# Expert stage of layer 0: an expert's 640 rows as units of 384 and 256 rows in place of twice 320

## What is computed

```python
capacity = max(1, int(T * CAPACITY_FACTOR / E))      # 2048 * 1.25 / 8 = 320
probs_full = jax.nn.softmax(xt @ Wr, axis=-1)
topv, topi = jax.lax.top_k(probs_full, TOPK)         # TOPK = 2
topv = topv / jnp.sum(topv, axis=-1, keepdims=True)
onehot = jax.nn.one_hot(topi, E, dtype=x.dtype)
rank = jnp.cumsum(onehot, axis=0)                    # per choice and expert
keep = (rank <= capacity).astype(x.dtype) * onehot
w = jnp.einsum('tk,tke->te', topv, keep)
h = jax.nn.gelu(jnp.einsum('td,edf->etf', xt, W1) + b1[:, None, :], approximate=False)
y = jnp.einsum('etf,efd->etd', h, W2) + b2[:, None, :]
out = jnp.einsum('te,etd->td', w, y)
```

## Time and profile before

| | us |
|---|---|
| median of three runs | 2173.74 |
| the three runs | 2163.47, 2173.74, 2173.80 |
| profiled execution, its own time | 2166.46 |
| its span, first to last instruction | 2164.7 |
| stage of the change, from the first `up` matmul to the first gather | 576.6 to 669.7 |

### The profile page before, as it was taken

The page is one execution under the profiler, slowest core; times in us unless marked ns, Lnnn a source line. Parts: engine busy times, 40 slices in busy tenths (PEclk is TensorE's granted clock), DMA queues, the critical chain, the costliest instruction groups (busy, mean ns, idle before and its releaser), DMA issues.

```text
span 2164.7 us, 31890 instructions
## 1 busy us (share of the span) xinstructions
PE 1946.3 (90%) x9894; PEld 1233.9 (57%) x9894; DVE 1432.5 (66%) x3907; ACT 966.6 (45%) x2009; POOL 1236.1 (57%) x1608
## 2 busy tenths in 40 slices
PE   5999999999794799999999988989699999898975
PEld 3655555555593465655655556777455555554554
DVE  6698688887243766666666544445578888876733
ACT  1445445444443435544544533545234445444443
POOL 1569977777453346766767700011256676798743
PEclk8899999999897889999999989999799999999987
DMA  5245132221423324434434220000312223222233
GB/s 138 65 108 146 46 81 50 59 58 41 136 74 82 73 59 103 98 75 98 98 79 93 65 81 20 1 12 1 80 43 70 53 52 84 61 66 71 54 102 97
DMA packets 126354, 155.59 MB, mean 72 GB/s; under 512 B 22136, under 2 KB 66456, under 8 KB 125928
## 3 DMA queue, kind: packets, MB, share of 16 engines
q1 hardware_dynamic: 121832, 145.43, 27.0%
q0 software_dynamic: 4352, 8.12, 1.2%
HBM read 47.84 MB, written 17.40 MB: 30 GB/s over the span
## 4 chain that ended last, share of the span: by engine, by line
PE 61%; DVE 12%; POOL 11%; issue 9%; ACT 4%; DMA 1%; SPq 0%; POOLq 0%; DVEq 0%; ACTq 0%
PE P L796 60%; POOL acc L1534 4%; POOL yd L1551 3%; DVE P L1924 2%; POOL xg L1542 1%; POOL acc L1531 1%; DVE mx L1913 1%; POOL pr L1512 1%; ACT pr L1302 1%; DMA xg<-xs,sidx 1%; DVE qB L1889 1%; DVE bst L1828 1%; PE P L823 0%; DVE mx L1924 0%; DVE mx L1934 0%
## 5 line engine op out<-in xcount | busy, mean ns | idle before, releaser
L1534 POOL TENSOR_TENSOR acc<-acc,pr 128x512 f32<-128x512 f32 (+3 forms) x768 | 676.5, 904 | 94.4 <-ACT pr L1302 70.1
L1302 ACT ACTIVATE pr<-P 128x512 f32<-128x512 f32 (+1 forms) x768 | 396.5, 567 | 398.3 <-PE P L796 388.7
L796 PE MATMUL P<-pr,vt 128*64 128x512 f32 (+3 forms) x2304 | 445.0, 507 | 5.1 <-POOL pr L1512 5.0
L796 PE MATMUL P<-qA,kA 128*128 128x512 f32 (+2 forms) x1024 | 413.1, 406 | 31.4 <-ACT pr L1302 31.0
L796 PE MATMUL P<-qB,kB 128*128 128x512 f32 (+2 forms) x1024 | 370.7, 367 | 0.0
L1512 POOL TENSOR_SCALAR_AFFINE_SELECT pr<-pr 128x256 f32<-128x256 f32 x384 | 156.7, 408 | 342.1 <-ACT pr L1302 305.1
L796 PEld LDWEIGHTS P<-qA,kA 128*128 128x128 f32 x1024 | 195.0, 190 | 160.6 <-issue 73.3
L796 PEld LDWEIGHTS P<-pr,vt 128*64 128x64 f32 x2304 | 146.8, 139 | 233.8 <-issue 195.5
L1913 DVE TENSOR_REDUCE mx<-P 128x1 f32<-128x512 f32 x384 | 243.8, 683 | 44.4 <-PE P L796 43.0
L1531 POOL TENSOR_TENSOR acc<-pr,pr 128x384 f32<-128x384 f32 x192 | 217.6, 1144 | 87.4 <-ACT pr L1302 87.2
L1924 DVE CUSTOM_DVE_ANT_0 P<-P,maskQ,mx 128x512 f32<-128x512 f32 (+3 forms) x384 | 190.0, 554 | 45.4 <-PE P L796 44.4
(11 more groups left out here) (331 smaller groups left out, 3196.4 us busy)
## 6 DMA issues: line engine op xcount, KB each, us to landing
qA<-hq SPq DMA_DIRECT2D x384, 128.0 KB
kA<-stage SPq DMA_DIRECT2D x168, 128.0 KB
qB<-qB SPq DMA_DIRECT2D x96, 128.0 KB
kB<-stage SPq DMA_DIRECT2D x84, 128.0 KB
nr<-null_share SPq DMA_DIRECT2D x64, 128.0 KB, 2.9
yd<-in_c_zero SPq DMA_DIRECT2D x32, 128.0 KB, 2.7
w<-in_L_W SPq DMA_DIRECT2D x16, 256.0 KB, 5.8
xg<-xg SPq DMA_DIRECT2D x24, 129.0 KB
```

Of the source, the lines that this page charges most:

```text
L796: return P.matmul(out, lhs, rhs, start=start, stop=stop)
L1302: S.activation(a.pr[slot][:, r, 512 - wide:512], m.bank[b][:, 512 - wide:512], AF.Exp, scale=0.125).then_inc(s.free[b], 1)
L1534: G.tensor_tensor(acc[:, sl], acc[:, sl], pt[:, sl], ALU.add).then_inc(s.acc, 1)
```

## The change

An expert's 640 rows stay where they are, with the same weights. Unit 2e now takes the first 384 of them, unit 2e+1 the last 256. The row tiles of a unit are then 128, 128, 128 or 128, 128. The third transpose, the third group of four `down` matmuls, the third part of the index and bias operations, the third scatter and the second row load exist for even units only. `up`, its Gelu and the `xt` copies have 384 or 256 columns. The `xt` and `h` buffers grow from 320 to 384 columns. The tables of the destinations, `c_base0` and `c_place0`, are made as before (with 320 rows for each unit), and so are all sizes of layer 3, whose counts of semaphores are only written in another form.

```diff
--- before.py
+++ after.py
@@ -15,7 +15,8 @@
...
 ROWS = {0: 16 * L0_CAP, 3: 8 * L3_CAP}
-CAP = {0: L0_CAP, 3: L3_CAP}
+SHARES = {0: (384, 256), 3: (L3_CAP,)}
 UNITS = {0: 16, 3: 8}
@@ -27,6 +28,19 @@
...
           3: (("Wq", 0, 512, "wq"), ("Wq", 512, 512, "wq"), ("Wk", 0, 64, "wk"))}
+
+def share(L, u):
+    return SHARES[L][u % len(SHARES[L])]
+
+def first_row(L, u):
+    return u // len(SHARES[L]) * sum(SHARES[L]) + sum(SHARES[L][:u % len(SHARES[L])])
+
+def row_tiles(L, u):
+    return [(o, min(128, share(L, u) - o)) for o in range(0, share(L, u), 128)]
 
@@ -579,7 +593,7 @@
...
     def experts(stack, L):
-        e, W, per = Box(), CAP[L], UNITS[L] // 8
+        e, W, per = Box(), max(SHARES[L]), UNITS[L] // 8
         e.raw = [sb(stack, f"w1raw{i}", [128, 512]) for i in range(3)]
@@ -1001,32 +1015,31 @@
...
                 L, u = k
-                W = CAP[L]
                 w.wait_ge(s.x_rows[u % 5], rows_count(L, u))
...
                 xg = m.E[L].xg[u % 5]
-                for t, (o, wd) in enumerate(((0, 128), (128, 128), (256, W - 256))):
+                for t, (o, wd) in enumerate(row_tiles(L, u)):
                     last = P.transpose(ps[:, o:o + wd], xg[0:wd, t, 0:D], m.ident[0:wd, 0:wd])
...
                 L, u, mt = k
-                e, W = m.E[L], CAP[L]
+                e, W = m.E[L], share(L, u)
                 ex = u // (UNITS[L] // 8)
...
                 ms = slice(mt * 128, mt * 128 + 128)
-                mm3(ps[:, 0:W], e.w1[ex % 4][0][:, ms], e.w1[ex % 4][1][:, ms], e.xt[u % 3][0][:], e.xt[u % 3][1][:],
+                mm3(ps[:, 0:W], e.w1[ex % 4][0][:, ms], e.w1[ex % 4][1][:, ms], e.xt[u % 3][0][:, 0:W], e.xt[u % 3][1][:, 0:W],
                     True, True).then_inc(s.full[b], 1)
...
                 L, u = k
-                e, W = m.E[L], CAP[L]
+                e = m.E[L]
                 ex = u // (UNITS[L] // 8)
...
                 w.wait_ge(s.free[b], uses)
-                for t, (o, wd) in enumerate(((0, 128), (128, 128), (256, W - 256))):
+                for t, (o, wd) in enumerate(row_tiles(L, u)):
                     for kk in range(4):
@@ -1165,7 +1178,8 @@
...
 
-    return 32 * (u // 5 + 1 + (0 if L == 0 else len([v for v in range(16) if v % 5 == u % 5])))
+    units = [(l, v) for l in (0, 3) for v in range(UNITS[l]) if v % 5 == u % 5 and (l, v) <= (L, u)]
+    return sum(32 if share(*unit) > 256 else 16 for unit in units)
 
@@ -1361,7 +1375,7 @@
...
                     w.wait_ge(*pl.filled("up", L, u - 3, 3))
-                S.copy(m.E[L].xt[u % 3][0][:].bitcast(FR), ps[:, 0:CAP[L]]).then_inc(s.e_x, 1)
+                S.copy(m.E[L].xt[u % 3][0][:, 0:share(L, u)].bitcast(FR), ps[:, 0:share(L, u)]).then_inc(s.e_x, 1)
             elif kind == "up":
@@ -1369,7 +1383,7 @@
...
                     w.wait_ge(*pl.filled("down", L, u - 3))
-                S.activation(e.h[u % 3][:, mt, :], ps[:, 0:CAP[L]], AF.Silu if L else AF.Gelu,
+                S.activation(e.h[u % 3][:, mt, 0:share(L, u)], ps[:, 0:share(L, u)], AF.Silu if L else AF.Gelu,
                              bias=e.b1[:, ex * 4 + mt:ex * 4 + mt + 1]).then_inc(s.free[b], 1)
@@ -1547,7 +1561,7 @@
...
                 w.wait_ge(s.e_to, od.nth("cols", L, u))
-                for t, wide in enumerate((128, 128, CAP[L] - 256)):
+                for t, (_, wide) in enumerate(row_tiles(L, u)):
                     G.indirect_dma_start(yd[L], bass.IndirectOffsetOnAxis(ap=e.ni[u % 4][0:wide, t:t + 1], axis=0),
@@ -1572,7 +1586,8 @@
...
 
-    return 48 * (u // 4 + 1 + (0 if L == 0 else 4))
+    units = [(l, v) for l in (0, 3) for v in range(UNITS[l]) if v % 4 == u % 4 and (l, v) <= (L, u)]
+    return sum(16 * len(row_tiles(*unit)) for unit in units)
 
@@ -1582,9 +1597,10 @@
...
     def rows_in(xg, L, u, sem):
-        W = CAP[L]
-        Y.dma_start(xg[:, 0:2, :], xgd[L][u * W:u * W + 256, :].rearrange("(t p) d -> p t d", p=128)).then_inc(sem, 16)
-        Y.dma_start(xg[0:W - 256, 2, :], xgd[L][u * W + 256:u * W + W, :]).then_inc(sem, 16)
+        o, W = first_row(L, u), share(L, u)
+        Y.dma_start(xg[:, 0:2, :], xgd[L][o:o + 256, :].rearrange("(t p) d -> p t d", p=128)).then_inc(sem, 16)
+        if W > 256:
+            Y.dma_start(xg[0:W - 256, 2, :], xgd[L][o + 256:o + W, :]).then_inc(sem, 16)
 
@@ -2159,14 +2175,14 @@
...
                 L, u = k
-                e, W = m.E[L], CAP[L]
+                e, W = m.E[L], share(L, u)
                 xg = e.xg[u % 5]
...
                     w.wait_ge(s.y_out[u % 4], y_count(L, u - 4))
-                parts = ((128, slice(0, 2)), (W - 256, slice(2, 3)))
+                parts = ((128, slice(0, 2)), (W - 256, slice(2, 3)))[:1 + (W > 256)]
                 for wd, c in parts:
@@ -2179,17 +2195,19 @@
...
                 w.wait_ge(s.e_x, od.nth(*item))
-                V.tensor_tensor(e.xt[u % 3][1][:].bitcast(FR), ps[:, 0:W], e.xt[u % 3][0][:], ALU.subtract).then_inc(s.free[b], 1)
+                V.tensor_tensor(e.xt[u % 3][1][:, 0:W].bitcast(FR), ps[:, 0:W], e.xt[u % 3][0][:, 0:W], ALU.subtract).then_inc(s.free[b], 1)
             elif kind == "down":
                 L, u = k
-                e, W = m.E[L], CAP[L]
+                e, W = m.E[L], share(L, u)
                 ex, y = u // (UNITS[L] // 8), e.y[u % 4]
...
                     w.wait_ge(s.y_out[u % 4], y_count(L, u - 4))
-                V.tensor_tensor(y[:, 0:2, :], ps[:, 0:256].rearrange("p (i n) -> p i n", i=2),
-                                e.b2[:, ex:ex + 1, :].broadcast_to([128, 2, 128]), ALU.add)
-                V.tensor_tensor(y[0:W - 256, 2, :], ps[0:W - 256, 256:384], e.b2[0:W - 256, ex, :], ALU.add).then_inc(s.free[b], 1)
+                last = V.tensor_tensor(y[:, 0:2, :], ps[:, 0:256].rearrange("p (i n) -> p i n", i=2),
+                                       e.b2[:, ex:ex + 1, :].broadcast_to([128, 2, 128]), ALU.add)
+                if W > 256:
+                    last = V.tensor_tensor(y[0:W - 256, 2, :], ps[0:W - 256, 256:384], e.b2[0:W - 256, ex, :], ALU.add)
+                last.then_inc(s.free[b], 1)
             elif kind == "comb":
```

## The result

The changed kernel takes 2156.52 us (median of 16 runs), beside 2166.53 us for the kernel before (16 runs on the same chip): a ratio of 0.9951, interval 0.9937 to 0.9965, so 10 us or 0.5% less. The forecast of 2157.7 is 1.2 us off, and that is luck: I took 16 us off the median of three runs, 2173.7, the median of sixteen lies 7 us lower, and the gain came out 6 us smaller. The two misses cancel.

The account below looks back on a forecast made before the run. PE was taken to bound the stage from the first `up` to the last `down`; 9.5 + 4.1 + 1.4 - 0.35 - 0.1 + 1.3 = 15.85, say 16 us, off 2173.74 gave 2157.7 us, range 2145 to 2168.

Parts of the forecast that it names:

- `down`, 9.5 us: `down` matmuls on PE: odd units 1.79 and even units 2.68 in place of 2.90 us; 9.5 us less.
- `cols`, 4.1 us: Transposes of units 2 to 15 on PE: 0.33 or 0.22 us in place of 0.57; 4.1 us less.
- `up`, 1.4 us: `up` matmuls on PE: 2.10 and 1.44 us against twice 1.86; 0.18 a pair, 1.4 us less in eight pairs.
- Pace: Steady units: a pair takes 8.56 us in place of 10.66, with POOL, ACT and the scatter's loop keeping up.
- the row of 24 records: Sign to look for in PE's timeline: an even unit's 24 `down` records in 2.95 us.
- Sum up to the 15th `down`, 14.65 us: PE's path to the 15th `down`: gains of 9.5, 4.1 and 1.4 us, less 0.35 for half clock at the start.
- rival B: A second engine takes back a third of the gain, early or in the index loop: 2163 us; chance 0.12.
- its second place: Rival B's index loop: its slack of 2 us spent by an unseen wait in DVE's or ACT's order.
- Its first place: Rival B early, where DMA is busy: PE would reach unit 3's rows some 0.5 us earlier.
- The end, 1.3 us: After the 15th `down`: POOL has five scatters in place of six, 1.26 us less.
- the slack of the scatter's loop: DVE's indices for unit u+4 wait for unit u's landing: loop 6.8 us, landing 2.1, leaving 2 us of slack.
- The start: Unit 0: 12 wider `up` matmuls at half clock take 0.7 us more (0.35 lost), DVE's `xtl` 0.1 more.

Follow-up runs that it names:

- narrow_m64: Changed kernel with `down` computing 64 rows in place of 128 in the third row tile of even units, counts unchanged; ratio to the kernel before 0.9952.
- wide_third: Kernel before, still 320 rows a unit, with every operand made full (third transpose rows 192 to 319, zero columns in `down`); ratio 0.9997.
- again: The changed kernel run once more, unedited, in a second comparison; ratio to the kernel before 0.9921.
- late_wld: Changed kernel with SP issuing the loads for layer 1 after unit 1 has started; ratio to the kernel before 0.9891.
- unique_place: Changed kernel with destinations made from each unit's real first row, so no two units share one for empty rows; ratio to the kernel before 0.9924.
- before_again: The kernel before, unedited, against itself; ratio 0.9991.
- before_deep5: Kernel before with five buffers in place of four for `nf`, `ni` and `y`; ratio 0.9995.
- deep5: Changed kernel with five buffers in place of four for `nf`, `ni` and `y`; ratio to the kernel before 0.9912.
- before: The kernel before the change, unedited, in its first profile; 2166.53 us (median of 16 runs).
- small_first: Changed kernel with 256 rows first, then 384, and unique destinations; ratio to the kernel before 0.9928.
- all_three: Changed kernel with five index and y buffers, `place` loaded first, and layer 1's loads issued after unit 1's start; ratio to the kernel before 0.9912, median 2147.28.

## Why the prediction was right, step by step

**`down`, 9.5 us.** Right: 2.68 and 1.79 us measured, as worked out. `narrow_m64` isolates the 0.22 of an even unit, `wide_third` the rest.

**`cols`, 4.1 us.** Right in sum. `cols` to `up` is 0.14 and 0.24 where I had 0.22 and 0.33, since `up` starts 0.03 us after the last transpose; the second `up` matmul then comes 0.26 after the first in place of 0.18, so the difference lands in `up`.

**`up`, 1.4 us.** 2.19 and 1.52 measured against 2.10 and 1.44, for that reason. `cols` and `up` of a pair together: 4.09, forecast 4.09. The rows of attention carried over.

**Pace.** 8.55 us for a pair, forecast 8.56. `wide_third` splits the 2.11 us that a pair gains: 1.14 are the shape's, and the rest are eight `down` records and one transpose fewer (8 x 0.112 + 0.11 = 1.0). The 2.95 us that the prediction gave for the row of 24 records was a slip: 23 x 0.112 + 0.27 are 2.85, and the row has 2.84.

**Sum up to the 15th `down`, 14.65 us.** From the earlier trace rows's first `up` to the last `down` are 86.41 us before and 71.92 after, 14.49 less, of which the 16th `down` itself is 1.11. That leaves 13.4; with the stall of 1.3 it is 14.7. The steady terms were right to 0.1 us, and the stall is what was missing: rival B, with its second place (`up` waits for `xtl`, the index loop), but with 1.3 us in place of 5. Its first place, unit 3's rows, cost 0.22 us here and 0.97 in `again`. The agreement to 0.1 is partly luck, for the first two units vary by 0.3 to 0.5 us between profiles of one kernel; the steady pairs (six of them, 12.7 us less without the stall, forecast 12.6) don't depend on that.

**The end, 1.3 us.** 1.1 measured: 14.48 us less to the last scatter, 13.4 to the 15th `down`.

**The step that failed: the slack of the scatter's loop.** I gave it 2 us, with a landing of 2.1. In steady work `xtl` starts 2.05 us before the `up` that needs it, against 0.65 where PE does wait for it, so the slack is 1.4: the loop from the end of `down` to `up` takes 7.3 us (1.1 to the first scatter, 2.5 to the last, 2.3 to the landing, 1.3 to the `up`) where I had 6.8, and `cols` adds 0.14 where I had 0.3. And in the stage's first 35 us the landing isn't 2.1 us: the wait ended 4.87, 4.57, 4.43 and 4.18 us after the last issue in the changed kernel, `again`, `late_wld` and `unique_place`. In the kernel before, `nf` starts 2.25 to 2.48 us after the last issue in eleven of twelve units (once 3.69, and 3.24 at the same unit in `before_again`). So one late landing was there to be read, harmless because the loop had 4 us of slack; the change made them frequent, and took the slack that hid them. `before_deep5` says the same: nothing to gain there.

**Why the landings are late.** Busy time by stretch, from the last issue to the landing (the last two columns are DMA share and GB/s). The kernel before, units 0 and 4:

```profile
590.30:592.70 2.40, 2.40 (x18) 1.87 (x17) 0.66 (x3) 0.43 (x1) 0.91 (x1) 1.00 0.25 78
...
611.20:613.50 2.30, 2.30 (x19) 1.77 (x17) 0.54 (x2) 0.00 (x0) 0.90 (x1) 1.00 0.48 146
```

The changed kernel, units 0, 2, 4 and 8:

```profile
589.00:593.90 4.90, 4.90 (x46) 4.89 (x44) 0.43 (x1) 1.95 (x5) 2.87 (x3) 1.00 0.58 180
...
598.40:600.80 2.40, 2.40 (x23) 2.40 (x22) 0.42 (x1) 1.08 (x3) 1.66 (x2) 1.00 0.53 164
...
607.20:610.80 3.60, 3.60 (x34) 3.60 (x33) 0.43 (x1) 2.47 (x6) 2.80 (x3) 1.00 0.78 240
...
624.40:626.70 2.30, 2.30 (x22) 2.30 (x21) 0.44 (x2) 1.32 (x4) 1.86 (x2) 1.00 0.19 57
```

The late ones in the changed kernel stand beside more traffic: the faster stage asks for its weights and rows more densely, and its scatters fall among them. But the share isn't the whole rule, for unit 2's landing took 2.39 us at 0.53. The Trainium skill (DMA: Bandwidth & Descriptors, SWDGE vs HWDGE vs iDMA) has both kinds of queue, GpSimd's and SP's, on the same engines, which take turns between them. These rows fit that but don't show it, and `late_wld` moved only a part of the weight transfers. Nor does traffic explain the one late landing of the kernel before (unit 10, 3.69 us), where the share was 0.12. The stretch, and a line of its DMA queues:

```profile
643.10:646.70 3.60, 3.60 (x28) 3.07 (x27) 0.61 (x2) 1.19 (x3) 1.74 (x2) 1.00 0.12 32
q8 instruction: 1, 0.02, 1.6%
```

Beside that scatter the DMA engines moved one packet of program code of 16 KB (644.64 to 645.56). Such a packet also falls beside the landings of 4.87 and 3.55 us in the changed kernel, 4.57 in `again`, 4.43 in `late_wld` and 4.18 in `unique_place`, while unit 2's stretch has none, and in unit 8's it had ended, at 625.29, before the scatter's own packets began at 625.89. A scatter lands in 16 parts, and where it is late by this, one part is: of unit 4's last scatter all recorded parts but one had landed 2.24 us after the issue, the last after 3.46; of the kernel before's unit 10, 2.13 and 3.60. It isn't the whole rule either: unit 0's other parts took up to 3.55 us, and `wide_third` has a landing of 3.84 us with no code packet, at a share of 0.77. So traffic and code packets are both supported and neither is shown, since no run moved either alone. Shown is that a landing can be late with no shared destination, and that a fifth buffer makes the late landings harmless.

**The start.** The first `up` of 12 matmuls at half clock took 4.18 us where the earlier trace rows had 3.54, 0.64 more, as forecast (0.7). From the last attention matmul to it are 7.67, 8.78 and 7.84 us in three profiles without the change (`before_deep5` the third), 8.59, 8.16, 8.64, 8.90 and 8.95 in five with it (`deep5`, `late_wld` and `unique_place` the last three): means of 8.10 and 8.65, 0.55 more. `xtl` is 0.08 of that. The rest lies in the landing of b1, b2 and `place`, for which DVE waits 4.2 to 5.0 us; the spread is as large as the difference. Here too code packets may play a part: one begins 1.5 to 1.9 us after the last attention matmul in `before_again` (8.78), the changed kernel's first profile, `deep5`, `late_wld` and `unique_place` (8.59 to 8.95), and none there in `before`, `before_deep5` and `again` (7.67, 7.84, 8.16); but `narrow_m64` and `wide_third` have 8.86 and 8.71 without one, and `small_first`, whose first unit has 256 rows, has 8.29 with one. Whether the 0.55 belongs to the change is open.

**The whole.** 14.4 to 14.7 us less in the stage and perhaps 0.55 more ahead of it make 14, a ratio of 0.9935: just below the first comparison's interval and inside the second's. The forecast of 16 was 2 us too much: 1.3 for the stall, 0.2 at the end and the rest ahead of the stage.

## What to carry to other kernels

Count what a changed operand shape costs by the steps between matmul starts: a tile of 64 in a stream of 128s cost nothing by its own duration, and 0.57 us a unit by the changes to and fro, so here the even shapes were worth half of the gain and the fewer instructions the other half. When the bound engine gets a fifth faster, look again at each loop over buffers with the longest landing in the trace, not the typical one; one more small buffer was enough. And judge a change of 0.5% by its stage in several profiles, with the medians only as a bound.

## What the runs showed of the hardware that was not expected

- Each change of TensorE's operand shape cost 0.14 us: in the trace the next start comes after 0.20 us and the one behind it after 0.16, in place of 0.11 (`narrow_m64`: 4.33 to 4.61 for two changes), and a unit with four changes lost 0.57 (`wide_third`: 5.33 to 4.76). The Trainium skill (TensorEngine Tiling (Array Packing), Key Properties) says that changing the tiling mode drains TensorE. The size is from these rows; that these shape changes are such changes of mode isn't shown.
- Weight loads last 191 ns at steps of 0.112 us, and in the changed kernel they are busy for 20.00 of 20 us, with no loss in the steps.
- A scatter of 128 rows of 512 bytes took from 2.3 to 4.9 us from its issue to its landing in one stage. One of its 16 parts can be 1.2 to 1.5 us behind all others, also where there is hardly other traffic (share 0.12).
- When every operand had full shape at 320 rows a unit, PE stood several times for up to 1.1 us with nothing that the trace names, in both profiles, and once for 0.72 us in `all_three`. The kernel before has no such row. This is open.
